# FP4 quantising in a four-block transformer kernel: the clamp moves to GpSimd, two small scale operations are folded into others

## The reference

```python
def fake_quant_nvfp4(x, global_scale):
    xb = x.reshape(sh[:-1] + (sh[-1] // BLOCK, BLOCK))        # BLOCK = 16
    amax = jnp.max(jnp.abs(xb), axis=-1, keepdims=True)
    sc = jnp.clip(amax / FP4_MAX * global_scale, 0.0, FP8_MAX)    # 6.0, 448.0
    sc8 = sc.astype(jnp.float8_e4m3fn).astype(jnp.float32)
    dq = sc8 / global_scale
    safe_dq = jnp.where(dq == 0.0, 1.0, dq)
    a = jnp.clip(jnp.abs(xb) / safe_dq, 0.0, FP4_MAX)
    q = jnp.sign(xb) * _FP4_VALS[jnp.digitize(a, _FP4_MIDS)]
    return (q * dq).reshape(sh)

s_w = FP8_MAX * FP4_MAX / max|w|          # per weight matrix; the inputs' scales are s_in, s_in_down
gate_out, up_out = linear(x, gate_w, s_in), linear(x, up_w, s_in)
hidden = jax.nn.silu(gate_out) * up_out                       # 1024 wide
out = linear(hidden, down_w, s_in_down)                       # both operands fake-quantised
```

## Time and profile before

| | us |
|---|---|
| three runs | 3251.67, 3260.39, 3262.79 |
| median | 3260.39 |
| the profiled execution | 3268.76, its span 3267.0 |
| DVE busy in the span | 1909.6 (58%) |
| PE busy in the span | 2732.1 (84%) |
| POOL busy in the span | 1078.9 (33%) |

### The profile page before, as it was taken

The page is one execution under the profiler, slowest core; times in us unless marked ns, Lnnn a source line. Parts: engine busy times, 40 slices in busy tenths (PEclk is TensorE's granted clock), DMA queues, the critical chain, the costliest instruction groups (busy, mean ns, idle before and its releaser), DMA issues. The chain is left out here.

```text
span 3267.0 us, 45506 instructions
## 1 busy us (share of the span) xinstructions
PE 2732.1 (84%) x17204; PEld 1570.5 (48%) x17204; DVE 1909.6 (58%) x3481; ACT 1469.3 (45%) x1978; POOL 1078.9 (33%) x980
## 2 busy tenths in 40 slices
PE   5888888869879899998878898898998996788544
PEld 3443433623345444445743444587787875333222
DVE  4655655667756544444666666644544433766688
ACT  2556556236732354455325555534333331466322
POOL 3223332223220255565217777620010111022333
PEclk7999997879989899999889999899999998789666
DMA  7566562055520011112000000002211212555000
GB/s 171 114 117 140 122 123 64 1 116 123 123 94 14 17 38 41 47 44 73 27 14 1 1 1 14 13 13 64 81 58 56 66 51 81 96 111 101 26 10 15
DMA packets 130376, 202.76 MB, mean 62 GB/s; under 512 B 36368, under 2 KB 66608, under 8 KB 129520
## 3 DMA queue, kind: packets, MB, share of 16 engines
q1 hardware_dynamic: 98416, 147.46, 19.5%
q0 software_dynamic: 31744, 52.41, 5.9%
HBM read 134.92 MB, written 64.78 MB: 61 GB/s over the span
## 5 line engine op out<-in xcount | busy, mean ns | idle before, releaser
L2383 DVE TENSOR_REDUCE L_mx<-bank_t 128x2 f32<-128x1024 f32 (+3 forms) x512 | 565.2, 1121 | 335.9 <-PE bank_t L2189 213.8
L2383 DVE TENSOR_REDUCE L2a_mx<-bank_t 128x2 f32<-128x1024 f32 x256 | 311.9, 1223 | 348.8 <-PE bank_t L2166 347.8
L2586 ACT ACTIVATE L_P<-bank_t 128x1024 f32<-128x1024 f32 (+3 forms) x384 | 340.3, 916 | 262.2 <-PE bank_t L2201 144.0
L2586 ACT ACTIVATE L2a_P<-bank_t 128x1024 f32<-128x1024 f32 x256 | 261.8, 1024 | 257.9 <-PE bank_t L2178 257.4
L2189 PE MATMUL bank_t<-L_KS,L_QS 48*128 48x512 f32 (+2 forms) x1024 | 243.2, 478 | 123.9 <-ACT L_P L2586 48.6
L2166 PE MATMUL bank_t<-L2a_QK 32*128 32x512 f32 x1536 | 253.9, 439 | 53.6 <-ACT L2a_P L2586 25.5
L2201 PE MATMUL bank_t<-L_QS,L_KS 50*128 50x512 f32 (+2 forms) x1024 | 244.9, 482 | 21.2 <-DVE L_mx L2383 12.6
L2174 PE MATMUL bank_t<-L2a_QK 32*128 32x512 f32 x1536 | 255.2, 443 | 0.0
L2166 PEld LDWEIGHTS bank_t<-L2a_QK 32*128 32x128 f32 x1536 | 136.9, 192 | 217.0 <-ACT L2a_P L2586 119.1
L2201 PEld LDWEIGHTS bank_t<-L_QS,L_KS 50*128 50x128 f32 x1024 | 101.2, 198 | 260.3 <-issue 174.6
L2231 PE MATMUL bank_o<-L_P,L_V 128*32 128x512 f32 (+3 forms) x1536 | 205.7, 612 | 8.8 <-ACT L_P L2586 6.1
(11 more groups left out here) (455 smaller groups left out, 5997.9 us busy)
## 6 DMA issues: line engine op xcount, KB each, us to landing
L_KS<-L_spill_k_halves SPq DMA_DIRECT2D x174, 128.0 KB, 5.6
L_QS<-L_spill_q_halves SPq DMA_DIRECT2D x174, 128.0 KB, 4.6
L_spill_raw<-xn POOLq DMA_DIRECT2D x64, 256.0 KB, 2.5
L2g_raw<-in_L_ffn_h_blocks SPq DMA_DIRECT2D x32, 512.0 KB, 3.8
L_spill_k_halves<-L_hi SPq DMA_DIRECT2D x32, 256.0 KB, 2.1
L_spill_k_halves<-L_lo SPq DMA_DIRECT2D x32, 256.0 KB, 2.4
L_spill_q_halves<-L_hi SPq DMA_DIRECT2D x32, 256.0 KB, 2.7
L_spill_q_halves<-L_lo SPq DMA_DIRECT2D x32, 256.0 KB, 3.1
```

The costliest lines, as they stand in the source:

```text
L2383: e.tensor_reduce(neg, s.tile[:, :, 0:n_keys], AX.X, ALU.max, negate=True).then_inc(sem(s.done), 1)
L2586: e.activation(s.at.Pr[s.pb][:, :, q0:S], s.tile[:, :, q0:S], ACT.Exp, scale=s.at.scale).then_inc(sem(s.exp), 1)
```

## The change

Three edits:

1. The clamp to ±6 leaves VectorE. GpSimd does it, in place, as a second instruction behind its scaling, and waits for its own scaling first. `GridSteps` keeps only the bitwise AND.
2. The nine small operations become seven. The first one takes the column (global scale / 6) and the minimum with 448 at once; the sixth takes the minimum with -2^-10 (the sign is no longer flipped) and multiplies by a column that holds the reciprocal of -(1 + 2^-22) times the global scale; the reciprocal behind it is then the last.
3. The columns are made beforehand. `L3f_cols` grows from 12 to 22 columns, two for each of the five global scales. For the three weight matrices the three operations stand inside `WeightScale`; for the two inputs a new step, `InputScales`, is added right behind the loads of `e_in`.

```diff
         def vector_program(dve):
+            def scaled_columns(j):
+                sixth, inverse = scale_cols[j]
+                e.tensor_scalar(sixth, col[:, j:j + 1], 1.0 / FP4_MAX, None, ALU.mult)
+                e.tensor_scalar(inverse, col[:, j:j + 1], -(1.0 + 2.0 ** -22), None, ALU.mult).then_inc(step.sem, 1)
+                dve.wait_ge(step.due())
+                return e.reciprocal(inverse, inverse)
...
             e_in = [load(col[:, 10:11], dram["L3_ffn_s_in"].to_broadcast([P, 1])),
                     load(col[:, 11:12], dram["L3_ffn_s_in_down"].to_broadcast([P, 1]))]
+            add(InputScales(e_in, due("input_scales_made")))
...
+                elif kind is InputScales:
+                    dve.wait_ge(*s.after)
+                    scaled_columns(10)
+                    scaled_columns(11).then_inc(sem(s.done), 1)
+                    dve.wait_ge(s.done)
...
                 elif kind is Quantise:
-                    e.tensor_scalar(am, am, 1.0 / FP4_MAX, s.gs, ALU.mult, ALU.mult).then_inc(step.sem, 1)
-                    dve.wait_ge(step.due())
-                    e.tensor_scalar(am, am, FP8_MAX, None, ALU.min).then_inc(step.sem, 1)
+                    e.tensor_scalar(am, am, s.gs[0], FP8_MAX, ALU.mult, ALU.min).then_inc(step.sem, 1)
...
-                    e.tensor_scalar(inv, sc8, -1.0, 2.0 ** -10, ALU.mult, ALU.max).then_inc(step.sem, 1)
+                    e.tensor_scalar(inv, sc8, -(2.0 ** -10), s.gs[1], ALU.min, ALU.mult).then_inc(step.sem, 1)
                     dve.wait_ge(step.due())
-                    e.reciprocal(inv, inv).then_inc(step.sem, 1)
-                    dve.wait_ge(step.due())
-                    e.tensor_scalar(inv, inv, s.gs, 1.0 + 2.0 ** -22, ALU.mult, ALU.mult).then_inc(sem(s.inv), 1)
+                    e.reciprocal(inv, inv).then_inc(sem(s.inv), 1)
                 elif kind is GridSteps:
-                    e.tensor_scalar(yy, yy, FP4_MAX, -FP4_MAX, ALU.min, ALU.max).then_inc(step.sem, 1)
-                    dve.wait_ge(step.due())
                     e.tensor_scalar(mm.bitcast(I32), yy.bitcast(I32), 0x7F800000, None,
...
                 elif kind is ScaleBlocks:      # gpsimd_program
                     e.tensor_tensor(blocks(s.q.y[s.s][:, 0:s.n]), blocks(s.src), ..., ALU.mult
-                                    ).then_inc(sem(s.done), 1)
+                                    ).then_inc(step.sem, 1)
+                    pool.wait_ge(step.due())
+                    yy = s.q.y[s.s][:, 0:s.n]
+                    e.tensor_scalar(yy, yy, FP4_MAX, -FP4_MAX, ALU.min, ALU.max).then_inc(sem(s.done), 1)
```

More of the change, by code:

```diff
@@ L133 @@
 Quantise = namedtuple("Quantise", "q n gs s maxed inv")
+InputScales = namedtuple("InputScales", "after done")
 ScaleBlocks = namedtuple("ScaleBlocks", "q src n s after done")
@@ L248, in build_program @@
         zero1 = sb(ctx, "zero1", [P, 1])
-        col = sb(ctx, "L3f_cols", [P, 12])
+        col = sb(ctx, "L3f_cols", [P, 22])
+        scale_cols = {j: (col[:, 12 + 2 * i:13 + 2 * i], col[:, 13 + 2 * i:14 + 2 * i]) for i, j in enumerate((1, 4, 7, 10, 11))}
         const_ready = due("constants_made")
@@ L1812, in build_program, with quantise @@
         fp4_stored, fp4_ready = [], {}
-        def quantise(q, src, n, gs, after):
+        def quantise(q, src, n, j, after):
             s = q.count % len(q.y)
@@ L1818, in quantise @@
             add(BlockMax(q, src, n, s, [*after, q.y_free[s]], e_max))
-            return dict(q=q, s=s, n=n, read=e_scaled, scales=Quantise(q, n, gs, s, e_max, e_inv),
+            return dict(q=q, s=s, n=n, read=e_scaled, scales=Quantise(q, n, scale_cols[j], s, e_max, e_inv),
                         scale=ScaleBlocks(q, src, n, s, [e_inv], e_scaled))
@@ L1926, in quantised_weights @@
                 r, e_raw = ahead.pop(0)
-                item = quantise(q, raw[r], S, col[:, 3 * w + 1:3 * w + 2], [e_raw, fp4_ready[n]])
+                item = quantise(q, raw[r], S, 3 * w + 1, [e_raw, fp4_ready[n]])
                 scales(item)
@@ L1965, in x_part @@
                     x_norm(b, f.tail.raw_free)
-                item = quantise(q4, xn[:, b % 2, :, :].rearrange("p t c -> p (t c)"), TB * C, col[:, 10:11], [normal[b]])
+                item = quantise(q4, xn[:, b % 2, :, :].rearrange("p t c -> p (t c)"), TB * C, 10, [normal[b]])
                 xn_free[b % 2] = item["read"]
@@ L1991, in down_part @@
                 s2 = t % 2
-                item = quantise(q4, hid[t % 3][:, :], FF, col[:, 11:12], [e_h])
+                item = quantise(q4, hid[t % 3][:, :], FF, 11, [e_h])
                 hid_free[t % 3] = item["read"]
@@ L2481, in vector_program @@
                     dve.wait_ge(step.due())
+                    scaled_columns(3 * s.i + 1).then_inc(step.sem, 1)
+                    dve.wait_ge(step.due())
                     e.tensor_tensor(c, g, s.col[:, s.s_in:s.s_in + 1], ALU.mult).then_inc(step.sem, 1)
@@ L2796, in gpsimd_program @@
                                     s.q.small[s.s][:, 3, 0:nb].unsqueeze(2).to_broadcast([P, nb, BLOCK]),
-                                    ALU.mult).then_inc(sem(s.done), 1)
+                                    ALU.mult).then_inc(step.sem, 1)
+                    pool.wait_ge(step.due())
+                    yy = s.q.y[s.s][:, 0:s.n]
+                    e.tensor_scalar(yy, yy, FP4_MAX, -FP4_MAX, ALU.min, ALU.max).then_inc(sem(s.done), 1)
                     pool.latest = s.done
```

## The result

| | kernel before | changed kernel |
|---|---|---|
| median of 8 runs each, us | 3258.79 (3247.66 to 3265.69) | 3238.23 (3224.34 to 3243.39) |
| profiled execution: own time / span / clock | 3268.76 / 3267.0 / 0.899 | 3240.47 / 3238.5 / 0.908 |
| ratio | | 0.9942, 95% interval 0.9921 to 0.9964 |

The changed kernel is faster by 18.8 us (11.7 to 25.7).

What follows compares the result with a forecast made beforehand. VectorE was taken to bound the last feed-forward's loop (19.17 of 20 us busy), TensorE the background stage (94.1 of 100). Loop -14.8 plus entry +5.8 is -9.0, against the median 3260.39 giving 3251 us; range 3243 to 3266.

Steps and rivals of the forecast that it cites:

- step 18: Last step of the last feed-forward's main loop: forecast to gain 0.2 us.
- step 4: A step of the main loop, counted as one of ten full steps gaining 1.17 us each.
- The attention: Between background stage and loop: only the tile at its end was considered, with a gain of nothing.
- The clamp's price: Clamp on GpSimd in the loop: estimated at 1.10 us, called the weakest number.
- Rivals 1 to 3: Clamp on GpSimd costs 1.36, 1.93 or 2.37 us, giving 3256, 3265 or 3272; chances 0.14, 0.12, 0.08.
- The hold by GpSimd: In the loop, a one-source VectorE operation is held while GpSimd works on a tile, ending 0.55 us after it.
- The small operations: Folding nine into seven on VectorE: 0.17 us before the reciprocal and 0.28 behind it, 0.45 a tile.
- TensorE's part: In the loop: 0.8 us taken off the gain, as the down product would end about when VectorE wants it.
- Rival 4: TensorE's down product comes late in the loop; half the ten full steps lose 0.9 us: 3256, chance 0.10.
- Loop as a whole: Main loop of the last feed-forward: step gains of 15.6 us less 0.8 for TensorE, -14.8 us.
- The entry: Start of the background stage: InputScales waits for a load, delaying the first matmul through to the end, +5.8 us.
- rival 5: More than forecast: load lands early (entry 3.9), clamp under 0.9, loop gives 17 us: 3247, chance 0.16.

Runs made afterwards that it cites:

- clamp_twice: The changed kernel with the clamp done twice in a row on GpSimd, the second changing no value: 3259.53 us, ratio 1.0024 to the kernel before.
- no_clamp: The changed kernel with the clamp left out on both engines: 3224.75 us against 3248.61 for the kernel before, ratio 0.9934.
- fold_only: The changed kernel with the clamp back on VectorE: 3246.68 us against 3252.3 for the kernel before, ratio 0.9992.
- late_columns: The changed kernel with InputScales put behind VectorE's first work of the background stage: 3226.83 us against 3252.3 for the kernel before, ratio 0.9925.
- late_again: The kernel of late_columns, unchanged, measured once more beside the changed kernel: 3225.96 us, ratio 0.9911 to the kernel before.

## Why the prediction was wrong, point by point

The sum had -9.0 us; the ratio gives -18.8. The steps that failed are terms of the sum. The loop was put at -14.8 and gave -20.0 on the mean of the profiles, mostly through step 18, step 4 and a loss to TensorE that didn't come. The attention was put at nothing, without a reason, and was 6.3 shorter. The rest is the median that the sum was set against. The loop and the entry alone would not have left the range: 3260.39 - 20.0 + 5.2 is 3245.6. It was the attention, whose cause stays open, and the base that took the time below 3243. Point by point:

**The clamp's price**: right. 1.10 us estimated, 1.04 measured. Rivals 1 to 3, which rested on 1.36, 1.93 and 2.37, fall with it. The half of the Trainium skill's rule ("GPSIMD Engine Reference", section 4.1 "Engine selection") on which rival 1 leaned is on operations with two inputs, and this one has one, so the runs say nothing against it. On the other half, "1-input is roughly line-rate", the trace has 1.02 ns an element for GpSimd, 1.5 times VectorE's 0.67.

**The hold by GpSimd** (0.55 us behind it), read from one row: right for the AND, shown by clamp_twice and no_clamp, which moved the multiplication's end by +1.13 and -0.82 and took the AND's end with it. Two things were missing. The smaller: 0.55 belongs to 1024 elements. An operation of VectorE with 256, 0.41 us when nothing holds it, was held by GpSimd far earlier in the changed kernel's trace and ended 0.15 behind it:

```profile
786.97 0.98 DVE L2344 TENSOR_SCALAR xn<-X,mv,rstd 128x256 f32<-128x256 f32 x1
```

```profile
786.52 1.28 POOL L2790 TENSOR_TENSOR L_OT<-L_back 128x512 f32<-128x512 f32 x1 [4.58 <-DMA L_back<-L_spill_rec]
```

The larger: whoever starts first is not held. That is **the step that failed for step 18**: the forecast had the AND held until 0.55 behind the multiplication and a gain of 0.2; the AND started 0.05 ahead of it, took 0.69 and the step gained 2.08. In no_clamp the order is the other one, and the step is 1.0 longer. Nothing but the tail stands behind that AND.

**The small operations**: 0.45 forecast, 0.51 measured (fold_only): in eight plain full steps that is 0.5 us more.

**TensorE's part**, 0.8 taken off the loop: failed. Gate-and-up and the down product came in time: VectorE has no new wait of more than 0.2 us for PE in full steps but step 6. That one waited for TensorE before; it takes 9.67 us in the first profile, where its wait for `bank_o` grew by 0.5 us, and 8.57 to 8.67 in the other three, where it waits for ScalarE alone. The 6.3 us of TensorE's work in a step were also a little high: from 3225.28 to 3231.41 they are 6.1. Rival 4 falls too.

**Step 4** was put down as any full step, 1.17; it gave 4.04 in the profile and some 2.8 on the mean of all profiles, since VectorE waits in it for TensorE, at one clock or the other, and for ScalarE. The forecast named the low clock in the loop, but put no band around this term.

**Loop as a whole**: -14.8 forecast. The profiles give a mean of 184.0 before and 164.1 after, -20.0. The 5.2 us between: step 18 1.9, step 4 1.6, TensorE's 0.8, the small operations 0.5; the rest is small gains in steps 0, 3, 6, 8 and 17 against a step 1 that lost 0.4 on the mean where nothing was forecast: VectorE's wait for the load of `L_rec` grew from 0.27 to some 2 us, by more than VectorE had gained.

**The entry**: +5.8 forecast. The first matmul waited 5.3 us longer, and 180 us into the background stage the eight profiles with the step at the entry are 5.2 us behind the ten without. The delay is still there when the stage is over: from TensorE's last work ahead of the entry to the attention's first activation behind the stage it is 557.5 to 560.7 us in the eight, 551.0 to 556.3 in the ten, 5.8 apart on the mean. The mechanism (a load waited for by an in-order queue, then nothing to hide it) and the size were right. By time alone: late_columns and late_again beat the changed kernel, by 11 us where the two ran beside each other.

**Nothing in the background stage**: right. PE is busy 93.58 of 100 us at 2500 to 2600 where it was 94.14.

**The base**: the sum was set against a median of three runs, 3260.39. The runs beside which the changed kernel was then measured have 3258.79, 1.6 lower. Longer sets of the same kernel gave 3252.3 (29 runs), 3253.9 (23), 3256.9 (26) and 3255.9 (26), 3.5 to 8.1 lower. So between 2 and 8 of the 12.8 us that the forecast was off are the base's. The ratio of runs made side by side doesn't contain them, and it still says twice the forecast's gain. The range should have carried a few us for the base.

**The attention**: 0 in the forecast; 6.3 us shorter on the mean of profiles. With it the terms make -20.0 + 5.2 - 6.3 = -21 us, without it -15 (with the 5.8 of the stage's end 0.6 less each); the four ratios (0.9942, 0.9946, 0.9948, 0.993) say -17 to -23. The times don't decide between the two.

So the chance of 0.16 that the forecast gave to "more than forecast" (rival 5, 3247) pointed the right way for reasons that didn't hold: neither did the load land early, nor was the clamp under 0.9.

## What to carry to other kernels

A new step that waits for a load belongs behind the first work of its stage in an in-order queue: moved by one `yield`, it turned 0.9946 into 0.9911 side by side, of which the profiles account for 5 to 6 us, and that is the fastest of the kernels that compute all of it. Moving a one-source elementwise operation from a full VectorE to a half-idle GpSimd was worth it here, 0.73 us a step, as long as GpSimd's last operation of the step ends 0.55 us before VectorE's next `tensor_scalar` of 1024 elements would end; from there on what is added on GpSimd is added to the step (clamp_twice: 1.13 us more there, a full step 1.12 longer). And when a range is drawn around a small difference, the spread of the median it starts from, and the steps that TensorE's clock sets, are terms like the others.

## What the runs showed of the hardware that was not expected

- The hold has an order, and doesn't touch every operation with one source, as the forecast had put it. A TENSOR_SCALAR of VectorE that starts during an operation of GpSimd on a tile ends a fixed time after it, however long it was held: 0.55 us with 1024 elements (AND 0.68 to 2.30 us), 0.15 with 256, 0.05 with 64. One that starts 0.05 us ahead takes its usual 0.69 us and makes GpSimd's 0.50 longer (1.93 to 2.44). So even one of 64 elements took 1.92 us. The maxima (TENSOR_REDUCE, one source in SBUF too) are not held: they took their 1.21 us in step 16 from 3209.53, wholly beside the multiplication of 3208.86 to 3210.79.
- Loop steps that VectorE paces repeat to 0.01 us over all profiles. Whole executions of one kernel spread by 29 us (3239.90 to 3269.12 in one set of 29). What the profiles show of this are stretches with the same instructions and a different granted clock, as the attention's 243.6 to 251.5 us at 0.89 and 0.88.
- The first rounding, 1.22 us behind the ninth small operation, takes 1.16 directly behind the reciprocal. Not explained.
